# Low-rank products of the first two chunks in f32 on column tiles, and three input blocks asked for earlier

## What is computed

```python
x = x + einsum('bct,bcd->bdt', x, W0[itok_B_0_15])            # mixes the 64 rows of a batch
x = x + einsum('bct,bcd->bdt', x, W1[itok_B_0_15])            # the same, other weights
x = x + x @ W2.T + 0.5 * (x @ lora_A[itok_B_0_2]) @ lora_B.T  # 1024 columns, rank 32, table of 5
x = x + x @ W3[itok_B_3_7].T                                  # 1024 x 1024, one of 8 per batch
```

## Time and profile before

| | us |
|---|---|
| median of 3 runs (lowest to highest) | 380.28 (378.86 to 380.5) |
| the profiled execution, whole | 378.7 |
| its span in the profile | 376.9 |
| TensorE (PE) busy | 370.4 (98%) |
| VectorE (DVE) busy | 276.7 (73%) |
| ScalarE (ACT) busy | 221.5 (59%) |
| GpSimd (POOL) busy | 122.8 (33%) |

### The profile page before, as it was taken

One profiled execution on the slowest core, in us unless ns is written; L12 is line 12 of the kernel. 1 busy time (PEld: TensorE's weight loads), 2 busy tenths in 40 slices (PEclk: granted clock), 3 DMA queues, 4 the chain that ended last, 5 costly groups with the idle time before them and its releaser, 6 DMA issues.

```text
span 376.9 us, 8088 instructions
## 1 busy us (share of the span) xinstructions
PE 370.4 (98%) x1918; PEld 305.5 (81%) x1919; DVE 276.7 (73%) x328; ACT 221.5 (59%) x308; POOL 122.8 (33%) x162
## 2 busy tenths in 40 slices
PE   8999999999999999999999999999999999999985
PEld 6788888888888888888888878888888888888874
DVE  3796988699889876466795487954689546899633
ACT  3689558575359370454485495735767357667523
POOL 0000050200120100035694444853348533587400
PEclk9999999999999999999999999999999999999998
DMA  7974905953995761065726227632276322862223
GB/s 252 422 300 171 388 0 192 363 183 120 250 245 142 206 194 76 20 241 190 226 81 202 62 58 251 201 84 58 59 271 195 98 60 58 270 202 92 62 64 86
DMA packets 17565, 63.10 MB, mean 167 GB/s; under 512 B 1939, under 2 KB 2131, under 8 KB 15059
## 3 DMA queue, kind: packets, MB, share of 16 engines
q1 hardware_dynamic: 16448, 57.61, 44.8%
q0 software_dynamic: 576, 4.19, 5.8%
q10 hardware_dynamic: 466, 0.44, 0.4%
HBM read 52.80 MB, written 8.39 MB: 162 GB/s over the span
## 4 chain that ended last, share of the span: by engine, by line
PE 97%; ACTq 1%; ACT 1%; issue 0%
PE ps L1787 45%; PE ps L1620 11%; PE ps L1621 11%; PE ps L1622 11%; PE ps L1813 4%; PE ps L1706 3%; PE ps L1879 2%; PE ps L1647 2%; PE ps L1679 2%; PE ps L1601 2%; PE ps L1602 2%; PE ps L1603 2%; PE ps L1663 1%; PE ps L1828 0%; ACT L802 0%
## 5 line engine op out<-in xcount | busy, mean ns | idle before, releaser
L1787 PE MATMUL ps<-ring,aT 128*128 x752 | 173.4, 389 | 0.0
L1787 PEld LDWEIGHTS ps<-ring,aT 128*128 128x128 f32 x752 | 141.1, 188 | 29.8 <-issue 0.6
L566 POOL TENSOR_TENSOR aT<-xT,aT 128x512 fp32r<-128x512 f32 (+1 forms) x36 | 56.6, 1593 | 42.2 <-ACT aT L920 37.5
L1620 PE MATMUL ps<-ring 128*128 128x512 f32 x176 | 68.8, 391 | 0.0
L1621 PE MATMUL ps<-ring 128*128 128x512 f32 x176 | 68.5, 389 | 0.0
L1622 PE MATMUL ps<-ring 128*128 128x512 f32 x176 | 68.5, 389 | 0.0
L1491 DVE TENSOR_TENSOR ring<-raw,ring 128x1024 f32 (+1 forms) x40 | 63.8, 1652 | 5.9 <-ACT ring L906 5.9
L926 ACT ACTIVATE aT<-ps 64x1024 fp32r<-64x1024 f32 x32 | 32.7, 1023 | 48.8 <-PE ps L1787 48.5
L1519 DVE TENSOR_TENSOR stage<-ps,stage 64x1024 f32<-64x1024 f32 x30 | 36.7, 1222 | 28.9 <-ACT stage L935 28.2
L1508 DVE TENSOR_TENSOR aT<-ps,aT 64x1024 fp32r<-64x1024 f32 x32 | 39.1, 1223 | 21.7 <-ACT aT L926 21.0
L935 ACT ACTIVATE stage<-ps 64x1024 f32<-64x1024 f32 x30 | 30.5, 1018 | 23.7 <-PE ps L1813 23.4
(11 more groups left out here) (143 smaller groups left out, 392.3 us busy)
## 6 DMA issues: line engine op xcount, KB each, us to landing
raw<-w3t SPq DMA_DIRECT2D x40, 512.0 KB, 4.6
out<-stage SPq DMA_DIRECT2D x30, 256.0 KB, 3.1
ring_f<-xt SPq DMA_DIRECT2D x6, 1024.0 KB, 6.7
xT<-xt SPq DMA_DIRECT2D x6, 1024.0 KB, 8.4
raw<-xt SPq DMA_DIRECT2D x5, 1024.0 KB, 7.0
ring_f<-wt SPq DMA_DIRECT2D x3, 1024.0 KB, 7.0
xT<-wt SPq DMA_DIRECT2D x2, 1024.0 KB, 16.9
raw<-xt POOLq DMA_DIRECT2D x2, 1024.0 KB, 8.4
```

The source lines that it names most:

```text
L566: pool.tensor_tensor(x3_split(i, ks, P + h * T, T), xT[:, ks, bass.ds(which[h] * T, T)], as_f32(x3_split(i, ks, h * T, T)), ALU.subtract). ...
L1620: pe.matmul(dst, hi_of(qw)[:, k, cs], hi_of(qx)[:, k, :], start=start and k == 0, stop=False, skip_group_check=True)
L1787: last = pe.matmul(acc(i)[:, n, :], x3_split(i, k, start, P), ring[:, bass.ds(off + (part * D + n * 512), 512)], start=(k == 0 and j == 0) ...
```

## The change

Chunks 0 and 1 now make their low rank as chunks 2 and 3 do: A in f32 on four column tiles, x raw, and the same evacuation (`low_cols`, `low_highs` with eight copies, `low_less`, `low_lows` with four copies). So raw x0 to x3 have homes (`x_home`) in which they are not overwritten by their low parts: x0, x1, x2 in blocks of `xT` and x3 in the raw half of ring place 2. The A table is loaded once, straight to its place, and not split; B11_0 is not loaded a second time, since x0's home is `b11`. SP asks for x3, `keep` (B22_0) and `stg` (B12_0) right behind `w2t`, ahead of its wait and of W22. GpSimd zeroes the unused quarter of `low_split` as its first operation. VectorE makes x3's low part, T3 and T2 ahead of `s2` and `s3`, and x4's low part ahead of w2's; ScalarE makes x3's high part ahead of the picks of A and x4's ahead of w2's.

The diff, cut to its core:

```diff
+    x_home = (b11, out_block(1, 1), out_block(1, 0), raw_of(2))
...
             def load_x(n, half, c):
-                if n >= 3:
-                    wait_l2(sp, x_before(n))
-                sp.dma_start(raw_of(x_slot(n)), x_block(half, c)).then_inc(s(f"x_in{n}"), 16)
+                sp.dma_start(x_home[n], x_block(half, c)).then_inc(s(f"x_in{n}"), 16)
...
             load_x(1, 1, 1)
-            sp.dma_start(a_raw, lora_a).then_inc(s("stg"), 16)
+            sp.dma_start(a_tab.rearrange("p l k r -> p (l k r)"), lora_a).then_inc(s("a_tab"), 16)
             load_x(2, 2, 0)
             sp.dma_start(b_raw, lora_b).then_inc(s("kw"), 16)
             load_w(1, 1, 2)
             sp.dma_start(w1t, w_block(2, 1)).then_inc(s("w1t"), 16)
             sp.dma_start(w2t, w_block(1, 1)).then_inc(s("w2t"), 16)
+            load_x(3, 2, 1)
 
             def load_later(half, c):
                 sp.dma_start(later, x_block(half, c)).then_inc(s("later"), 16)
 
+            load_keep(2)
+            load_stg(1, 2)
             sp.wait_ge(s("b_split"), 4)
             sp.wait_ge(s("leaf_b"), 3)
             load_kw(w_block(2, 2))
-            load_x(3, 2, 1)
-            load_keep(2)
-            sp.wait_ge(s("a_tab"), 2)
-            load_stg(1, 2)
-            sp.dma_start(b11, x_block(1, 0)).then_inc(s("b11"), 16)
             sp.wait_ge(s("seed"), HALF)
             sp.dma_start(t4_of(0), x_block(2, 0)).then_inc(s("B21_0"), 16)
             wait_l2(sp, ("C11", 1, 3))
...
-            sp.wait_ge(s("a_sel0"), 2 * CP)
-            sp.wait_ge(s("a_sel"), 2 * CP)
-            sp.dma_start(a_tab_f.rearrange("p l k r -> p (l k r)"), lora_a).then_inc(s("a_tab_f"), 16)
...
+            pool.memset(low_split[R:2 * R, :, :].bitcast(F32), 0.0).then_inc(s("low_zero"), 1)
+            pool.wait_ge(s("low_zero"), 1)
...
-            wait_l2(pool, split_free(0))
-            pool.memset(low_split[R:2 * R, :, :].bitcast(F32), 0.0).then_inc(s("low_zero"), 1)
-            pool.wait_ge(s("low_lo"), LOW_LO[-1])
...
-            def select(pair):
-
-                if pair >= SEL:
-                    wait_l2(act, ("low", (pair - SEL) // CP, (pair - SEL) % CP))
-                for h in range(2):
-                    b = 2 * pair + h
-                    l = act.value_load(toks[0:1, 1, b:b + 1], min_val=0, max_val=NL - 1)
-                    act.activation(a_sel[:, pair % SEL, :, h, :, :].rearrange("p k t r -> p k (t r)"),
-                                   as_f32(a_tab[:, bass.ds(l, 1), :, :, :].rearrange("p l k t r -> p (l k) (t r)")),
-                                   ACT.Copy).then_inc(s("a_sel"), 1)
-
-            def select_f(b):
+            def select(b):
 
                 l = act.value_load(toks[0:1, 1, b:b + 1], min_val=0, max_val=NL - 1)
-                act.activation(a_sel_f[:, b - B // 2, :, :].rearrange("p k r -> p (k r)"),
-                               a_tab_f[:, bass.ds(l, 1), :, :].rearrange("p l k r -> p (l k r)"), ACT.Copy).then_inc(s("a_sel"), 1)
-
-            def low_out_whole(c):
+                act.activation(a_sel[:, b % (B // 2), :, :].rearrange("p k r -> p (k r)"),
+                               a_tab[:, bass.ds(l, 1), :, :].rearrange("p l k r -> p (l k r)"), ACT.Copy).then_inc(s("a_sel"), 1)
...
+            def low_out(c):
+                low_cols(c)
+                low_highs(c)
+
+            def low_cols(c):
+                wait_l2(act, ("low", c, 1))
+                act.activation(low_whole[:, 0, :], ps_low[:, c % 2, 0:P], ACT.Copy).then_inc(s("low_cols"), 1)
+
+            def low_highs(c):
                 j = c % 2
-                wait_l2(act, ("low", c, 1))
-                act.activation(low_whole[:, 0, :], ps_low[:, j, 0:P], ACT.Copy).then_inc(s("low_cols"), 1)
-                wait_l2(act, split_free(j))
+                if c >= 2:
+                    wait_l2(act, split_free(j))
                 act.wait_ge(s("low_cols"), c + 1)
                 for dst in (0, 3):
                     for i in range(GROUP):
                         act.activation(of_group(low_split[R * dst:R * (dst + 1), j, :], i),
                                        in_groups(as_f32(low_whole[R * i:R * (i + 1), 0, :])), ACT.Copy).then_inc(s("low_hi"), 1)
-
...
             x_loaded(1)
-            act.wait_ge(s("stg"), in_stg("a"))
-            act.activation(a_tab[:, :, :, 0, :].rearrange("p l k r -> p (l k) r"),
-                           a_raw.rearrange("p (a r) -> p a r", r=R), ACT.Copy).then_inc(s("a_tab"), 1)
             x_loaded(2)
 
             act.wait_ge(s("mm"), 2)
@@ -830,20 +792,21 @@
             act.wait_ge(s("leaf_b"), 1)
             act.activation(leaf_b[:, :], leaf_b_raw, ACT.Copy, scale=0.5).then_inc(s("leaf_b"), 1)
             low_highs(0)
-            act.wait_ge(s("a_tab"), 2)
+            act.wait_ge(s("a_tab"), 16)
             act.wait_ge(s("toks"), 16)
             t1(1, first_two)
-            for pair in range(4, 7):
-                select(pair)
+            x_loaded(3)
+            for b in range(CB, 2 * CB - 2):
+                select(b)
             c11(0, first_two)
-            select(7)
-            x_loaded(3)
+            for b in range(2 * CB - 2, 2 * CB):
+                select(b)
             c11(0, last_two)
             seed(0, first_two)
             t1(1, last_two)
             low_out(1)
+            x_from(4, stg, "T2", 1)
             w_from(2, kw, "S2", 3)
-            x_from(4, stg, "T2", 1)
             c11(1, first_two)
             seed(0, last_two)
             x_from(5, keep, "T3", 1)
@@ -851,7 +814,7 @@
             w_from(3, w2t, "S3", HALF + 1)
             u2(0, first_two)
             act.wait_ge(s("A22"), HALF)
-            wait_l2(act, ("low", 1, 3))
+            wait_l2(act, ("low", 1, 1))
             for name in ("A22", "A12", "A11"):
                 leaf_w_hi(name)
             u2(0, (2,))
...
             def t2(j):
 
                 dve.wait_ge(s("T3"), j + 1)
-                if j == 0:
-                    dve.wait_ge(s("b11"), 16)
-                else:
+                if j:
                     dve.wait_ge(s("stg"), in_stg("B11_1"))
                 dve.tensor_tensor(stg, stg if j else b11, keep, ALU.add).then_inc(s("T2"), 1)
...
-            def low_sum(c):
-                v = low[:, :].rearrange("p (j n) -> p j n", n=P)
+            def low_less(c):
                 dve.wait_ge(s("low_cols"), c + 1)
-                dve.tensor_tensor(v, low_parts_of(0), v, ALU.add).then_inc(s("low_sum"), 1)
+                dve.tensor_tensor(low_whole[:, 1, :], ps_low[:, c % 2, 0:P], as_f32(low_whole[:, 0, :]), ALU.subtract)\
+                   .then_inc(s("low_sum"), 1)
 
             def low_lows(c):
-                for h, src in ((0, 0), (1, 2)):
-                    dve.wait_ge(s("low_hi"), 5 * c + h + 1)
-                    rows = slice(R * src, R * (src + 1))
-                    dve.tensor_tensor(of_batch(low_split[2 * R:3 * R, c % 2, :], h), of_batch(low[rows, :], h),
-                                      as_f32(of_batch(low_split[rows, c % 2, :], h)), ALU.subtract).then_inc(s("low_lo"), 1)
-
-            def low_parts_whole(c):
                 j = c % 2
-                dve.wait_ge(s("low_cols"), c + 1)
-                dve.tensor_tensor(low_whole[:, 1, :], ps_low[:, j, 0:P], as_f32(low_whole[:, 0, :]), ALU.subtract)\
-                   .then_inc(s("low_sum"), 1)
-                wait_l2(dve, split_free(j))
+                if c >= 2:
+                    wait_l2(dve, split_free(j))
                 dve.wait_ge(s("low_sum"), c + 1)
                 for i in range(GROUP):
                     dve.tensor_copy(of_group(low_split[2 * R:3 * R, j, :], i),
                                     in_groups(as_f32(low_whole[R * i:R * (i + 1), 1, :]))).then_inc(s("low_lo"), 1)
 
             def low_parts(c):
-                low_sum(c)
+                low_less(c)
                 low_lows(c)
 
...
-            x_los(1)
-            dve.wait_ge(s("a_tab"), 1)
-            dve.tensor_tensor(a_tab[:, :, :, 1, :].rearrange("p l k r -> p (l k) r"), a_raw.rearrange("p (a r) -> p a r", r=R),
-                              as_f32(a_tab[:, :, :, 0, :].rearrange("p l k r -> p (l k) r")), ALU.subtract).then_inc(s("a_tab"), 1)
-            x_los(2)
...
-            dve.wait_ge(s("a_tab"), 2)
+            x_los(1, x_home[1])
+            x_los(2, x_home[2])
+
+            dve.wait_ge(s("a_tab"), 16)
             for b, l in enumerate(loras):
-                dve.tensor_copy(a_sel[:, b // 2, :, b % 2, :, :].rearrange("p k t r -> p k (t r)"),
-                                as_f32(a_tab[:, bass.ds(l, 1), :, :, :].rearrange("p l k t r -> p (l k) (t r)")))\
-                   .then_inc(s("a_sel0"), 1)
+                dve.tensor_copy(a_sel[:, b, :, :].rearrange("p k r -> p (k r)"),
+                                a_tab[:, bass.ds(l, 1), :, :].rearrange("p l k r -> p (l k r)")).then_inc(s("a_sel0"), 1)
             w_los(1, raw_of(w_slot(1)))
```

(30 more changed lines are left out.)

86 lines of the change are left out of this document (30 added, 56 removed).

## The result

The changed kernel takes 375.12 us (median of 4, 373.65 to 379.95), the kernel before 380.29 (378.86 to 380.5): a ratio of 0.987, 95% interval 0.984 to 0.989, faster by 5.2 us, where 3.4 were predicted. The execution that was profiled took 374.7, its span 372.9 against 376.9.

What follows compares the result with a forecast made beforehand. The prediction took TensorE to bound the kernel (busy 370.4 of 376.9 us). Two low-rank blocks saving 1.72 us each, nothing added, took the median from 380.28 to 376.9 us; range 375.4 to 379.8.

Steps and rivals of the forecast that it cites:

- Parts 1 to 5: Chunks 0 and 1: low rank saves 1.72 us each on TensorE; VectorE, ScalarE and loads are ready in time.
- the picks: VectorE's eight picks of A for chunk 0, halved to 256 elements: 0.25 us each taken, 0.35 as bound.
- estimate of 3.2 us for a block: Low rank of chunks 0 and 1 at 60 cycles a matmul, 128 records: saving 0.45 us per chunk, time 379.4.
- the sum: Whole kernel: 3.44 us off TensorE, nothing added; span 373.5, profiled execution 375.3, median 376.9 us.
- the 1.6: The kernel before's median lies 1.6 us above its profiled execution; the forecast carried that over to the changed kernel.
- Rival A: Column tiles pay less in chunks 0 and 1: 380.3 us at the bound, 378.6 halfway; chance 0.06.
- Rival B: TensorE is faster, then waits at x6, keeping 0.5 us of 3.44: 379.8 us; chance 0.11.
- Part 6: After chunk 1: later loads, leaves and chunks follow TensorE; x6 is the closest need; slots start 3.44 us earlier.
- the prediction's own signs of being right: Two 128-record blocks of some 2.1 us, no idle TensorE before 176, chain 97% TensorE, busy time 3.4 us less.
- Rival C: Three blocks asked for early slow w1's load, stalling TensorE in chunk 0 up to 7.0 us: 383.9 us; chance 0.07.

Runs made afterwards that it cites:

- Run 12: The kernel before the change, run once more with nothing changed, one execution: 380.16 us.
- run 2: The changed kernel with the 64 low-rank matmuls made twice in chunks 0 and 1: 387.98 us.
- run 6: The changed kernel with 9 warming matmuls of 512 columns in place of 18 of 256: 379.7 us.
- run 9: The changed kernel with 54 warming matmuls of 86 columns in place of 18 of 256: 375.96 us, ratio 0.991.
- run 3: The changed kernel's new low rank, but with loads and ScalarE's and VectorE's order as in the kernel before: 378.53 us, ratio 0.995.
- Run 7: The changed kernel with x3, keep, stg, w1t and w2t asked for only when chunk 0's low rank is done: 380.24 us, ratio 1.003.

## Why the prediction was right and wrong

**Parts 1 to 5 held.** The blocks cost 2.12 us each, so 3.44 were saved. The times listed above were within 0.6 us of the forecast; the picks were cheaper (0.21 us each, bound 0.35), and ScalarE's first C11 copy came at 35.99 (36.0). Chunk 1's four copies cost 1.75 us in place of 0.9, beside four operations of GpSimd (48.01 to 49.74), in a margin that took it. The estimate of 3.2 us for a block, worked out from the figure of about 60 cycles a matmul in the Trainium skill, TensorEngine Tiling (Array Packing), section Instruction Overhead, stood against 2.12 measured here as well.

**The step that failed is the sum**, "3.44 us off TensorE, nothing added". It took all that follows as moving with the block. In the profiled executions it gained 1.14 us more, the idle time before the last slot, which stood in the trace of before with no work as its cause and which the prediction did not count, and lost 0.67 at L4. With the 0.08 at the start that makes 3.44 + 0.08 − 0.67 + 1.14 = 4.0, which is what the profiled executions differ by (378.7 and 374.7). The other 1.2 us lie between these and the medians: before's is 1.6 above its profiled execution, after's 0.4 above its own. The prediction took the 1.6 for both. They are not just a matter of four executions: the changed kernel's eight executions in the lower group have a median of 374.4, 5.1 us under the kernel before's 379.6. Run 12 shows where an ordinary execution of before is longer, above all 0.9 us at the first slots, in a wait for GpSimd. Three of the profiled executions of the changed program or its versions have that wait as well (0.54 to 0.70 us, all with a stop in chunk 0), so why the lower group is spared is open, and so is why the last slot's idle time comes and goes with the program.

**And the result was luck.** 375.12 is the lower group's time. The median of all executions on record, 379.4, is 2.5 us above the forecast, on its other side.

**Rival A** did not happen. **Rival B** did in its form, at another place: TensorE came earlier and waited for VectorE, not at x6 but at L4, for 0.67 us and not for 3.0, and not in every execution. Part 6 had said of the leaves only that they hang on TensorE's events. U3 stands behind low parts in VectorE's order too. With it two of the prediction's own signs of being right failed: there is an idle row of TensorE at 118.6, before 176, and the chain is 92% TensorE and not 97%.

**Rival C** took the wrong victim. The early blocks did not slow w1. TensorE's instructions come over the same 16 engines, and they were late. That they stop TensorE is shown: the stop moves with the place in the program (runs 2, 6, 9) and ends 2.4 to 2.6 us behind the packet. That queued input delays the packet is shown in one trace, run 2's: 3.8 us from the start of the block to the packet under full engines, 0.6 with nothing else under way. Run 7's profiled execution (packet at 20.9 with less queued) agrees. But the engines were as full in the executions that didn't stop (share 1.05 while the packet of the kernel after started, at 22.25), so what decides between 22.25 and 26.75 in one and the same program is open. The three early blocks aren't needed for two groups, by run 3. No rival held this, and it cost 5 to 6 us in most executions. The four executions that make up the result caught it once. By its mechanism the changed kernel gains 5 us or nothing, and the median of a few runs can be either. In the old low rank the same supply was ample: 32 records in 3.84 us, against 128 in 1.93.

The Trainium skill, Runtime: NRT & Kernel Launch, section Instruction fetch mechanics, has TensorE's instructions refilled in blocks of 16 KiB, 256 instructions, by a DMA queue of its own, and calls the crossing mostly hidden. The trace agrees on the size (16 KB a packet; stops 128 matmuls and their 128 weight loads apart) and disagrees on the cost where a block is used up in two microseconds: 1.06 us with idle DMA engines (run 2), 2.9 to 3.8 us beside full data queues, and some 1.5 us more where the clock fell. The section also says that a taken branch outside the loaded window forces a fetch. The last slot's products stand behind a branch, which fits the 1.14 us; no run took the branch away, and the kernel after has the same branch and no idle time there.

## What to carry to other kernels

Many small matmuls are cheap for the array and dear for the instruction supply: count the instructions per microsecond, and when a low-cost block uses up some 256 of them in two or three microseconds, above all while input loads fill the DMA engines, look for an idle time marked "issue" in the middle of it and for when the instruction queue's packets come. Where the block of instructions ends can be moved with instructions that cost little, such as more and narrower warming matmuls. And when a change's times lie in two groups, profile one of each before believing a median.
